# Sixteen-row denominators in the gated cross-attention, and the order of the work up to the MX feed-forward

## The reference

```python
# x is layer-normalised before each block
q = query @ Wq.T
gate = jax.nn.sigmoid(query @ Wg.T + bg)
k, v = jnp.split(kv @ Wkv.T, 2, axis=-1)
q = feature_map(q)            # x > 0: x + 1, else exp(x); heads split
k = feature_map(k)
kv_summary = jnp.einsum('bhsd,bhse->bhde', k, v)
k_sum = k.sum(axis=-2)
z = 1.0 / (jnp.einsum('bhld,bhd->bhl', q, k_sum)[..., None] + 1e-6)
attn = jnp.einsum('bhld,bhde->bhle', q, kv_summary) * z
x = x + attn * gate @ Wo.T
# then, with both operands of each product dequantised MX blocks of 32:
x = x + mx_linear(silu(mx_linear(x, gate_w)) * mx_linear(x, up_w), down_w)
```

## Time and profile before

| what | value |
|---|---|
| time, median of 3 runs | 1945.07 us (1944.83 to 1945.47) |
| the profiled execution's own time | 1949.54 us |
| its span | 1947.8 us, so 1.74 us lie around it |
| mean granted PE clock | 0.979 |
| busy: PE, DVE, ACT, POOL | 1845.8, 1275.5, 701.8, 403.4 us |
| queries start | 1548.27 us |
| output products start | 1608.47 us |
| step 0 of the feed-forward starts | 1637.57 us |
| step 8 starts | 1706.26 us |

### The profile page before, as it was taken

How to read it: one execution, slowest core, us unless ns; L and a number is a source line. 1 busy time by engine, 2 the same in 40 slices (tenths; PEclk the granted TensorE clock), 3 DMA queues, 4 the chain that set the end, 5 groups by cost and what they waited for, 6 DMA issues and landing times. The chain is left out here.

```text
span 1947.8 us, 24670 instructions
## 1 busy us (share of the span) xinstructions
PE 1845.8 (95%) x9304; PEld 1384.6 (71%) x9304; DVE 1275.5 (65%) x2133; ACT 701.8 (36%) x1123; POOL 403.4 (21%) x306
## 2 busy tenths in 40 slices
PE   7999999899999999989999999999989999799998
PEld 5777886444443568758888888888878875678887
DVE  5334755665761666676787787687763398866766
ACT  3302232344445468733342342342334331212211
POOL 0000100211200258720121121111200011443532
PEclk9999998999999899999999999999999999899999
DMA  5102222232321311133122222313212100101101
GB/s 217 44 0 70 87 71 51 54 74 69 81 68 29 102 66 65 44 115 97 64 92 76 93 88 100 97 60 117 92 35 76 65 23 22 60 28 44 44 1 43
DMA packets 90374, 132.57 MB, mean 68 GB/s; under 512 B 11264, under 2 KB 54272, under 8 KB 88720
## 3 DMA queue, kind: packets, MB, share of 16 engines
q1 hardware_dynamic: 90256, 131.00, 21.4%
HBM read 97.21 MB, written 14.75 MB: 57 GB/s over the span
## 5 line engine op out<-in xcount | busy, mean ns | idle before, releaser
L802 DVE TENSOR_REDUCE b_nm<-ps 128x1 f32<-128x1024 f32 x128 | 153.1, 1219 | 91.1 <-PE ps L790 91.1
L1288 ACT ACTIVATE b_pr<-ps 128x512 f32<-128x512 f32 x256 | 133.5, 603 | 135.4 <-PE ps L1200 135.2
L248 PE MATMUL ps<-d_x_high,d_w_high 128*128 128x512 f32 x384 | 154.6, 403 | 1.7 <-issue 1.7
L249 PE MATMUL ps<-d_x_low,d_w_high 128*128 128x512 f32 x384 | 149.9, 390 | 0.0
L250 PE MATMUL ps<-d_x_high,d_w_low 128*128 128x512 f32 x384 | 149.9, 390 | 0.0
L2249 POOL TENSOR_TENSOR d_sqsum<-d_sqsum,d_sq 128x512 f32<-128x512 f32 x32 | 46.1, 1445 | 467.8 <-ACT d_sq L2161 467.5
L1212 PE MATMUL ps<-b_pr,b_VS 128*64 128x512 f32 x512 | 131.2, 636 | 0.0
L1745 POOL TENSOR_TENSOR c_h<-c_h,c_w_row 128x512 f32<-128x512 f32 x64 | 105.7, 1657 | 50.5 <-DMA c_w_row<-w_rows 27.8
L1200 PEld LDWEIGHTS ps<-b_qS,b_kS 98*128 98x128 f32 x256 | 44.1, 193 | 78.5 <-issue 52.3
L1200 PE MATMUL ps<-b_qS,b_kS 98*128 98x512 f32 x256 | 93.2, 447 | 6.9 <-ACT b_pr L1288 3.5
L790 PE MATMUL ps<-b_kS,b_qS 96*128 96x512 f32 x256 | 82.7, 408 | 5.9 <-DVE b_nm L802 4.5
(11 more groups left out here) (441 smaller groups left out, 5027.8 us busy)
## 6 DMA issues: line engine op xcount, KB each, us to landing
b_kS<-b_k_parts SPq DMA_DIRECT2D x96, 128.0 KB, 2.3
f_rows<-d_fw SPq DMA_DIRECT2D x24, 512.0 KB, 2.8
f_w<-f_rows SPq DMA_DIRECT2D x12, 1024.0 KB, 4.8
c_w_row<-w_rows SPq DMA_DIRECT2D x16, 512.0 KB, 3.5
b_qS<-b_q_parts SPq DMA_DIRECT2D x96, 64.0 KB, 2.0
a_convT<-in_convT SPq DMA_DIRECT2D x4, 1024.0 KB, 13.1
d_w<-in_d_wq SPq DMA_DIRECT2D x16, 256.0 KB, 2.8
d_w<-in_d_wk SPq DMA_DIRECT2D x16, 256.0 KB, 3.0
```

The source lines that it names most:

```text
L248: nc.tensor.matmul(out, lhsT[0], rhs[0], start=start, stop=False)
L249: nc.tensor.matmul(out, lhsT[0], rhs[1], start=False, stop=False)
L802: nc.vector.tensor_reduce(nm[:, g % 2, u:u + 1], c.ps[:, banks:banks + 2, :], AX.XY, ALU.max, negate=True).then_inc(job_read, 1)
L1288: nc.scalar.activation(pr[:, n % RING, :], c.ps[:, 4 + n % BANKS, :], ACT.Exp).then_inc(exp_done, 1)
```

## The change

In words, in the order of the program:
- The key sums now have 16 columns, one for a head (`e.ksum`, times a new table `e_heads`). `denominators(b)` is four accumulating float32 matmuls into 16 rows of one bank, once for each half of the tokens: behind the fifth query and behind the first gate.
- DVE adds 1e-6 and inverts 16 x 512 values, twice in all. ACT and DVE split the inverse in a high and a low part (`high_inverse`, `low_inverse`), and PE spreads it over 128 rows again: `spread_inverse(j)`, two matmuls with a 16-row operand for each job, eight jobs. `e_gz` is now that bank times the gate.
- Jobs go in pairs: two gates, two spreads, two numerators. The output products of tiles 0 and 1 stand behind the numerators of jobs 4 and 5, those of tiles 2 and 3 behind jobs 6 and 7, in banks 4 and 5. Their additions and measurements move on DVE too.
- The first eight weight tiles are turned four at a time, and their low parts move from POOL to DVE (`low_turned`).
- `unit_scales(1)` moves from step 0 to behind output tile 5, and `unit_scales(2)` and `unit_scales(3)` from steps 2 and 4 to steps 0 and 2. The low parts of token tiles 0 and 1 move from behind tile 5 to behind tile 6.
- `W_CHUNK` turns the tiles 8 to 19 as 1, 1, 1, 3, 2, 2 and 2 in steps 1 to 7. Hidden unit 0 is rounded in step 5 in place of step 6.
- Two small DMAs bring the tables `e_heads` and `e_headsT`, ahead of the output weights and ahead of the feed-forward's.

```diff
-        self.ksum = c.at("e_ksum", [P, 2, KD, P], F32, 112)
+        self.ksum = c.at("e_ksum", [P, 2, KD, 16], F32, 112)
...
-        self.z = c.at("e_z", [P, 2 * KD, BANK], F32, 132)
+        self.z = c.at("e_z", [16, 2, BANK], F32, 132)
...
+    W_CHUNK = {1: 1, 2: 1, 3: 1, 4: 3, 5: 2, 6: 2, 7: 2}
...
-        if s == 5:
-            return [], [], fresh
-        return fresh[:len(fresh) // 2], fresh[len(fresh) // 2:], []
+        return fresh[:(len(fresh) + 1) // 2], fresh[(len(fresh) + 1) // 2:], []
...
-    ROUNDED_AT = {2 * u + 6: [u] for u in range(STEPS // 2 - 3)} | {STEPS - 2 + i: [STEPS // 2 - 4 + i] for i in range(1, 4)}
+    ROUNDED_AT = ({5: [0]} | {2 * u + 6: [u] for u in range(1, STEPS // 2 - 3)}
+                  | {STEPS - 2 + i: [STEPS // 2 - 4 + i] for i in range(1, 4)})
...
-            lows(range(W_FIRST))
...
+            def gate_over_z(j):
+                b, m = JOBS[j]
+                dve.wait_ge(gate_ready, j + 1)
+                dve.wait_ge(spread_done, j + 1)
+                if j >= 2:
+                    dve.wait_ge(ag_done, j - 1)
+                nc.vector.tensor_tensor(e.gz[:, j % 2, :], c.ps[:, j % 2, :], e.gF[:, m, tokens(b)], ALU.mult).then_inc(gz_done, 1)
...
+            for i in range(NJ // 2):
+                units = range(KD * i, KD * (i + 1)) if i < 2 else []
+                turn_weights(units)
+                if i == 0:
+                    inverse(1)
+                    low_inverse(1)
+                elif i == 3:
+                    for t in range(2):
+                        add_gated(t)
+                        measure(t)
+                for j in (2 * i, 2 * i + 1):
+                    gate_over_z(j)
+                for j in (2 * i, 2 * i + 1):
+                    gated(j)
+                for u in units:
+                    low_turned(u)
+            for t in range(2, TT):
+                add_gated(t)
...
                 if t == 2:
                     unit_scales(0)
                 elif t == 5:
+                    unit_scales(1)
+                elif t == 6:
                     for r in FIRST:
                         low(r)
...
                 if s in (0, 2, 4):
-                    unit_scales(1 + s // 2)
                     unit_round(1 + s // 2)
+                    if s < 4:
+                        unit_scales(2 + s // 2)
...
+            def denominators(b):
+                pe.wait_ge(q_ready, KD * (b + 1))
+                for m in range(KD):
+                    last = nc.tensor.matmul(c.ps[0:16, b, :], e.ksum[:, b, m, :], e.qF[:, m, tokens(b)],
+                                            start=m == 0, stop=m == KD - 1)
+                last.then_inc(den_done, 1)
...
+                for part in range(2):
+                    last = nc.tensor.matmul(c.ps[:, j % 2, :], e.headsT[:, m, :], e.z_parts[part][:, b, :],
+                                            start=part == 0, stop=part == 1)
+                last.then_inc(spread_done, 1)
...
+            for i in range(NJ // 2):
+                gate(2 * i)
+                if i == 0:
+                    denominators(1)
+                gate(2 * i + 1)
...
+                for j in (2 * i, 2 * i + 1):
+                    spread_inverse(j)
+                for j in (2 * i, 2 * i + 1):
+                    numerator(j)
...
+                if i >= 2:
+                    for t in (2 * i - 4, 2 * i - 3):
+                        project(t)
```

More of the change, by code:

```diff
@@ L2988, in _, with gate @@
                 last.then_inc(q_done, 1)
[L2989 removed]
+                if j == 4:
                     pe.wait_ge(kv_ready, 2 * NJ)
[L2991 to L2993 removed]
+                    denominators(0)
+            def gate(j):
+                n, m = JOBS[j]
                 if j >= 2:
                     pe.wait_ge(gate_ready, j - 1)
[L2996 removed]
                 for k in range(KD):
@@ L3011, in _ @@
                         turn(r)
-                if t >= 2:
-                    pe.wait_ge(e_added, t - 1)
-                for k in range(KD):
-                    last = nc.tensor.matmul(c.ps[:, 6 + t % 2, :], e.gF[:, k, t * P:(t + 1) * P], e.woT[:, k, :],
-                                            start=k == 0, stop=k == KD - 1)
-                last.then_inc(e_out_done, 1)
+                project(t)
+            pe.wait_ge(ag_done, NJ)
             for s in range(STEPS + LAG):
@@ L3073, in _ @@
                                      bias=e.bg[:, m:m + 1]).then_inc(gate_ready, 1)
-                high_turned(j)
+                if j == 1:
+                    high_inverse(1)
+                if j in (1, 3):
+                    for i in range(2 * j - 2, 2 * j + 2):
+                        high_turned(i)
             for r in FIRST:
```

132 lines of the change are left out of this document (77 added, 55 removed).

## The result

The changed kernel takes 1951.24 us (median of 6 runs, 1947.13 to 1952.7) where the kernel before takes 1944.59 (median of 6, 1941.28 to 1945.47): ratio 1.0033, 95% interval 1.0022 to 1.0044, so 6.6 us slower. A second series on another occasion gave 1949.23 (12 runs) against 1945.21 (35 runs), 4.0 us slower by the medians; its ratio is 1.0024, interval 1.0015 to 1.0033. So the change makes the kernel slower, clear of the noise in both series. The forecast was 1946.1, range 1940.5 to 1951, with a chance of 0.51 for no change and 0.28 for slower by over 0.2%; the 1951.24 lies just outside that range.

A forecast was written before the change was run, and what follows sets the result against it. PE was taken as the bound from step 8 on, whose start POOL's queue set; DVE's order of work would set it after. Step 8 +1.0 us made 1949.5 into 1950.5, less 4.5 excess gave 1946.1, range 1940.5 to 1951.

The forecast's parts named there:

- The sum: Whole kernel: profiled 1949.5 becomes 1950.5; subtracting that execution's 4.5 us above the median gives 1946.1.
- the walk: From the cross-attention to step 8: work and waits of PE and DVE added up, step 8 opening at 1709.2.
- the same correction for step 8: Start of step 8 before the change: half clock lost 1.9 us, so the comparison is with 1708.2, not 1706.26.
- the cross-attention: Up to the third output product: spreads add 3.7 us, 2.1 and 0.4 come off; it ends 1.0 us later, at 1620.0.
- Fewer changes between formats give 0.4: PE in the cross-attention: fewer format switches between matmuls save 0.4 us.
- To step 0: Feed-forward step 0: DVE work of 22.6 us from 1620.0 makes it start at 1642.6, 5 us later.
- To step 6: Feed-forward step 6: DVE work of 44.1 us plus waits of 7.9 makes it start at 1694.6, 9 us later.
- To step 8: Feed-forward step 8: opens at 1709.2 at full clock, PE waiting 1.1 us, +1.0 us against 1708.2.
- The faster case: Feed-forward up to step 8: waits between ACT, POOL and DVE 2 us, not 7.9; 1940.2 us, chance 20%.
- The slower case: Feed-forward steps 1 to 5: four more POOL lows stop DVE, 5.1 us longer; 1951 us, chance 23%.
- Spreads at the float32 rate: Cross-attention on PE: each 16-row spread matmul costs a float32 pass, 3.2 us more; 1949.3 us, chance 5%.

The follow-up runs named there:

- the fresh 396.0: New trace of the kernel before, no edit: 396.0 us from the queries' start to the end; median 1944.84 us, ratio to before 0.9994.
- spread_pool: Kernel before with weight turns spread, unit_scales(2) and (3) in steps 0 and 2, their multiplications on POOL: 1940.58 us, ratio to before 0.9989.
- tables_only: Kernel before's cross-attention with the changed order from output tile 5 on and changed tables for weight turns and rounding: 1946.21 us, ratio to before 1.0010.
- high_spread: Changed kernel without the low part of the spread inverse, eight of sixteen matmuls left out: 1947.39 us, ratio to before 1.0021.

## Why the prediction was wrong, step by step

- **The step that failed is "The sum": "its own time is 4.5 above the median of 1945.07, so I forecast 1946.1".** It took the excess of one execution as a constant around the whole, which the changed kernel would shed like the old one. The excess was half clock at certain places: 3.5 us behind the queries, of which 2.9 in step 2, and 5 to 7 ahead of them. Step 2 lies within the stretch that the walk builds anew, and the walk has no half clock there. The prediction had the row (0.51 for 6.3 us) and made the same correction for step 8 (1.9 us), but for step 2 it put the term at nothing, without a reason. So its +1.0 came from a comparison that was already some 3 us too kind, and subtracting the excess counted this a second time. The forecast's own walk, 160.9 us from the queries to step 8 and 239.7 behind it, makes 400.6, which is +4.6 against the fresh 396.0.
- **The second term that was off is the cross-attention: mechanism right, size wrong (1.0 for 3.1).** The spreads cost 0.23 each, as priced, but the terms around them were too small. Four spreads take 1.12 us, not 0.93 (+0.8 over four groups). Two numerators behind them take 1.82, not 1.73 (+0.4 over four groups). A group of denominators lasts 3.53 where 3.47 stand by the price (+0.1 over two). 0.2 is the rounding from 1.2 down to 1.0. "Fewer changes between formats give 0.4" can't be found in any row (+0.4). Together these are 1.9 of the 2.1 us. They are readings of the timeline; only the spread's own price was tested by a run.
- **Both together.** The measured difference of like traces is 402.5 - 396.0 = +6.5: the forecast's +1.0, the 3.5 of the base and the 2.1 of the attention make 6.6. Against before's mixture of 396.0 and 399.5 it is +3.0 to +6.5; the 4.0 of the second series lies within, the 6.6 of the first at its end. The profiled 1950.61 of the changed kernel was close to its medians. That the third addition came at 1620.24 for a forecast 1620.0 was luck: the execution reached its queries 1.93 us earlier, which hid the 2.1.
- **To step 0, 5 us later:** right. From the third addition to step 0 it takes 22.63 us, forecast 22.6, with a wait of 3.60.
- **To step 6, nearly 9 us later:** right as a walk, 74.4 us behind the third addition (forecast 74.6), with its parts. The product h waits for the silu behind a single turned tile three times, 1.18 us each (1.2 forecast). The rounding waits 1.45 for POOL (1.8). Pairs beside POOL lose 1.0 at L2608 and, at L2595, 0.8 and 0.7 (1.07 and 1.02 for 0.29), 2.5 where 1.9 was forecast.
- **To step 8:** right, 88.9 us behind the third addition (forecast 89.2), at full clock behind 1.17 us. What I had as a fact of the change as a whole, that the hidden work moved ahead of step 6, is now shown for the rounding: moving it back gains 4.8 us to step 8.
- **The rivals.** The faster case ("the waits hardly arise") is out by the rows of h. The slower case came out in time, 1951, but not by its mechanism: the pairs of the roundings in steps 2 and 4 keep their 0.75 us, and POOL costs DVE 0.6 us more than forecast, not 5.1. Spreads at the float32 rate are out.

What stays open: which parts of the mixture of clocks each kernel has. With one trace for most kernels I can't say how often step 2 is at half clock. It was in one trace of before out of three, and it was in all three traces in which the turns are spread and step 0 is early, where PE waits 2.60 to 4.22 us at step 2 in place of 0.98. Whether this is the longer wait or the draw, a second trace of each would tell. For the same reason the worth of the early scales inside the changed kernel, and of an early step 0 in spread_pool, isn't settled. Nor is it tested why the early rounding and the spread turns hurt together: spreading the turns gains 4 us with the rounding in step 6, while with the rounding in step 5 undoing the spread makes step 8 2.1 us earlier.

## What to carry to other kernels

Before a profiled execution is used as the base of a sum, see where its excess over the median lies: if it is lost clock, it belongs to places, and a change that rebuilds such a place takes it along or not. Compare stretches, not totals; cut at a fixed event, two executions of one kernel agree within 0.1 us where the clock is the same, while totals of this kernel differed by up to 10. Work moved ahead in an engine's list is free only where that engine would have waited; ask at each place who waits for whom, since here the same rounding costs 4.8 us more ahead of step 6 than behind it. And a relief of an engine that is not the bound in its stretch bought nothing here (the cross-attention), while an idle engine (POOL) that took work from the one that is the bound (DVE, ahead of step 6) brought step 8 1.9 and 2.9 us forward in the two kernels where it was tried with late step 0.

## What the runs showed of the hardware

- The same wait is followed by full clock in one execution and by half clock in another. Ahead of step 2 PE waited 1.6 and 0.98 us in all traces of before; the clock behind it was 0.51 over 6.3 us once and 1.00 twice. TensorE: Matmul & The Clock Gate of the Trainium skill (What's actually happening) says that the gate looks at PE on its own beat, independent of the kernel's start; the traces agree. So part of the clock's loss differs from one execution to the next: 12 executions of before spread over 9.3 us, 1939.23 to 1948.48, with mean granted clocks of 0.985 down to 0.980.
- Waits of 3.60 and 10.22 us were followed by half clock (0.61 and 0.54), waits of 1.72, 2.10 and 1.17 by full clock, in both traces of the changed kernel. That is no rule: ahead of step 4 of tables_only PE waited 2.07 us, and the clock behind it was 0.64 over 4.7 us. It cost nothing there, since DVE sets step 6: from step 4 to step 6 it took 22.29 us, and 22.28 in the changed kernel at full clock.
- A split matmul with 16 operand rows and 512 columns takes 0.23 us, as one with 128 rows does (high_spread).
- An inversion of 16 x 512 takes as long as one of 128 x 512 on DVE: the row below, against 3.31 in the earlier trace rows.

```profile
1579.15 3.34 DVE L2851 RECIPROCAL e_z<-e_z 16x512 f32<-16x512 f32 x1
```
